# Two transformer graph layers: three stages replaced by one unrolled loop with a chunked softmax and zero matmuls

## Chip, cores and metric

The kernel runs on one core of a Trainium2 chip. The metric is device time in microseconds. Times are given as the median of the runs shown; the profile is of one further execution. TensorE's clock has two levels in these traces, 1.2 and 2.4 GHz, shown as a granted clock of 0.50 and 1.00.

## What is computed

Four graph networks in sequence on 3125 nodes with 128 features and 50,000 edges (`src`, `dst`), each followed by a residual and a layer norm: relation convolution, GCN, GATv2, and two transformer convolutions. The change concerns the last two:

```python
def transformer_conv(x, edge_index, Wq, bq, Wk, bk, Wv, bv, Ws, bs):   # H = 4 heads, C = 32
    q, k, v = (x @ Wq + bq), (x @ Wk + bk), (x @ Wv + bv)              # each N x H x C
    alpha = einsum('ehc,ehc->eh', q[dst], k[src]) / sqrt(C)
    amax = segment_max(alpha, dst)
    ealpha = exp(alpha - amax[dst])
    denom = segment_sum(ealpha, dst)
    out = segment_sum((ealpha / denom[dst])[..., None] * v[src], dst)
    return out.reshape(N, H * C) + x @ Ws + bs
h = relu(transformer_conv(x, ...)); out = transformer_conv(h, ...)
```

## The kernel before

The edges are sorted into 416 pairs. A pair is up to 128 edges (one per partition) whose destinations lie in one window of 125 nodes; there are 25 windows. `m.pair_src` and `m.pair_dst` hold source row and destination inside the window, `m.pair_win_i` the window. Four pairs (G = 4) are a group: 104 groups. What a pair needs of its destination nodes is fetched, and what it gives them is added, by a matmul with a one-hot matrix of edges against nodes.

Each transformer layer is five blocks one after the other (`build`, L1857). `conv_nodes` (L1691) computes q, k, v and the skip part and writes k and v to `kv_table` in DRAM. Then:

- `conv_scores` (L1735). GpSimd gathers k and v rows, one indirect DMA for each pair, into eight slots of `got` (L917); it may run eight groups ahead and waits for a slot's reader. SyncE puts the v half aside into `v_rows` (L938). VectorE makes bf16 one-hots `hot` (L927); TensorE transposes them (L1801), ScalarE copies them to `hot_t` as f32 (L1787), and TensorE multiplies them with q to give `q_b` (L1814; an f32 matmul is two passes, so four pairs are eight instructions). VectorE multiplies `q_b` by the gathered k (L1775), reduces (L1778) and scales (L1780). `q_b`, `hot_b` and `hot_t` have two buffers each.
- `segment_softmax` (L94): the maximum of each destination over all 416 pairs and four heads (1664 columns) by transposes, scans and two broadcasting matmuls (L131), then exp.
- `conv_sums` (L1007), in groups of eight pairs: load `v_rows` back, one-hots `hot` (L1064), messages `msg` = v times weight (L1068), and on TensorE the sums: an f32 matmul with the message (L1092), a bf16 matmul of 12 columns with the weights in three bf16 parts (L1093), and after every second pair a 512-column bf16 matmul of zeros (L1097). The next group's vector work runs beside them.
- `conv_finish` (L1819) divides and adds.

Each engine works through its own list in order; semaphores order the engines among each other. `segment_softmax` is also used by the GAT layer, `gcn_nodes` (L835) prepares the GCN layer.

Of the kernel before, what the change touches and what calls it, by code (L numbers as in the profile page):

```python
# [20 lines left out]
Q, W = 125, 25  # L21
# [9 lines left out]
YS, Y_EARLY, SL = 6, 6, 24  # L31
# [5 lines left out]
assert TILES * P >= E and FULL + W <= PAIRS and Q * W == N  # L37
# [51 lines left out]

def nodes(ap):  # L90
    return ap.rearrange("(w q) d -> q w d", q=Q)

def segment_softmax(nc, m, acc=None):  # L94
# [3 lines left out]
    with ExitStack() as ctx:  # L98
# [12 lines left out]
        alpha = m.alpha[:, :, :].rearrange("l h p -> l (h p)")  # L111
# [34 lines left out]
        def _(dve):  # L146
# [12 lines left out]
            link(v.tensor_copy(topf, high[:, 0:cols]))  # L159
# [18 lines left out]
            link(v.tensor_tensor(less, m.alpha[:, :, :], top[:, :, :], ALU.subtract))  # L178
# [7 lines left out]
def common(m, sb):  # L186
# [14 lines left out]
    m.alpha = sb("alpha", [P, H, PAIRS])  # L201
# [307 lines left out]
def relation_layer(nc, m, y_table):  # L509

    with ExitStack() as ctx:  # L511
# [19 lines left out]
        same = m.alpha  # L531
        pens = m.small[:, :, :].rearrange("l p k -> l (p k)")
        start_pen, end_pen = (pens[:, k * H * PAIRS:(k + 1) * H * PAIRS].rearrange("l (h p) -> l h p", h=H) for k in range(2))
# [32 lines left out]
        def _(dve):  # L566
# [69 lines left out]
            for h in range(H):  # L636
                go(v.tensor_copy(start_pen[:, h, :], ps[2][:, 0:PAIRS]))
                go(v.tensor_copy(end_pen[:, h, :], ps[3][:, 0:PAIRS]))
# [22 lines left out]
            go(v.tensor_scalar(m.leader[:, :], start_pen[:, 0, :], -1.0, None, ALU.is_lt))  # L661
# [69 lines left out]
        def _(pe):  # L731
# [40 lines left out]
            for k, pen in enumerate((start_pen, end_pen)):  # L772
                flat = pen[:, :, :].rearrange("l h p -> l (h p)")
# [61 lines left out]
def gcn_nodes(nc, m, ins, t_table):  # L835

    with ExitStack() as ctx:
# [4 lines left out]
        tb, hb = [bank(f"t1{i}") for i in range(2)], [bank(f"h1{i}") for i in range(4)]  # L842
        loaded, chain, var_ready, std_ready, x_ready = (sem(n) for n in ("loaded1", "chain1", "var1", "std1", "x1_ready"))
# [4 lines left out]
        def _(sp):  # L848
            sp.dma_start(w1[:, :], ins["L1_gnn_W"]).then_inc(loaded, 16)
            for w in range(0, W, 5):  # L850
                sp.wait_ge(t_ready, w + 5)
                sp.dma_start(nodes(t_table)[:, w:w + 5, :], tmp[:, w:w + 5, :]).then_inc(stored, 16)
            sp.wait_ge(stored, 16 * (W // 5))

# [8 lines left out]

        @block.scalar
        def _(act):
            std_of(nc, act, stats, var_ready, std_ready, 1)
# [6 lines left out]
        def _(pe):  # L873
            pe.wait_ge(x_ready, 1)
# [130 lines left out]

def conv_sums(nc, m, v_rows):  # L1007

    with ExitStack() as ctx:  # L1010
        sb, sem, bank = scope(nc, ctx)
        zeros = sb("zeros", [P, 512], BF16)
        rows = sb("rows", [P, 2, WG, D])
        hot = sb("hot", [P, 2, WG, Q])
        msg = sb("msg", [P, 2, WG, D])
        wts = sb("wts", [P, 2, WG, H])
        hot_b, wts3 = sb("hot_b", [P, 2, WG, Q], BF16), sb("wts3", [P, 2, WG, 3, H], BF16)
        left, zero = sb("left", [P, 2, WG, H]), sb("zero", [P, WG, H])
        sums = bank("sums", (P, 8 * 512))
        dens = 7 * 512  # L1020
        used, zeroed, done, hot_ready, wts_ready, msg_ready = (sem(n) for n in (
            "used", "zeroed", "all_summed", "hot_ready", "wts_ready", "msg_ready"))
        hot_b_ready, parts_ready, chain, zero_ready = (sem(n) for n in ("hot_b_ready", "parts_ready", "parts_chain", "zero_ready"))
        come = [sem("come0"), sem("come1")]
        steps = PAIRS // (2 * WG)
        block = ctx.enter_context(nc.Block())

        @block.sync
        def _(sp):  # L1030
            with sp.Fori(0, steps) as i:
                for b in range(2):
                    sp.wait_ge(msg_ready, 2 * i + (b + 1))
                    sp.dma_start(rows[:, b, :, :].rearrange("l (a j) d -> l a (j d)", a=2),
                                 v_rows[bass.ds(i * 4 + 2 * b, 2), :, :].rearrange("a l n -> l a n")).then_inc(come[b], 16)

        @block.gpsimd
        def _(pool):
            pool.memset(zero[:, :, :], 0.0).then_inc(zero_ready, 1)
            pool.wait_ge(zero_ready, 1)  # L1040
            with pool.Fori(0, steps) as i:
                for b in range(2):
                    g = 2 * i + b
                    pool.wait_ge(wts_ready, g + 1)
                    three_parts(pool, wts3[:, b, :, :, :], wts[:, b, :, :], left[:, b, :, :], zero[:, :, :], chain, g, parts_ready)

        @block.scalar
        def _(act):
            with act.Fori(0, steps) as i:
                for b in range(2):  # L1050
                    act.wait_ge(hot_ready, 2 * i + (b + 1))
                    nc.scalar.copy(hot_b[:, b, :, :], hot[:, b, :, :]).then_inc(hot_b_ready, 1)

        @block.vector
        def _(dve):
            v = nc.vector
# [678 lines left out]
def conv_scores(nc, m, kv_table, v_rows):  # L1735

    with ExitStack() as ctx:
# [24 lines left out]
        def _(dve):  # L1763
            v = nc.vector
            dve.sem_inc(used, 2)
            for b in range(2):
                loop.one_hots(b * G, b)
# [156 lines left out]
```

## Time and profile before

| | us |
|---|---|
| median of three runs | 4879.6 (4878.93 to 4885.05) |
| the profiled execution | 4863.76 |
| its span, first to last instruction | 4862.0 |
| mean granted clock over the span | 0.716 |

The page's busy line counts an engine as busy while an instruction runs; waits, register and semaphore instructions are not in it. Its strips cut the span into 40 slices of 121.5 us. The transformer layers are the slices from the 27th on. A table by stretches says more than the whole-span shares, because the stages have different limits; in the timelines and groups the bracket or the third column is the idle time before an instruction and what ended it.

### The profile page before, as it was taken

To read this page: it belongs to the slowest core of one execution; us is meant where nothing else is said; L and a number is where in the kernel's file an instruction comes from. 1 tells how busy PE (TensorE), PEld (TensorE's weight loads), DVE (VectorE), ACT (ScalarE), POOL (GpSimd) and SP (SyncE) were. 2 spreads that over 40 slices of the span, in tenths; PEclk is the share of its full clock that TensorE was granted. 3 is DMA by queue.
4 is the path that set the end of the run, shared out by engine and by line. 5 is a ranking of instruction groups with operands and counts; after the bars stand their busy time and mean duration, and the time that the engine had idled before them with its cause. 6 is when DMAs were issued, how large, how long until landed. Compare 5 with 4: busy or idle time off the path is not lost. (4 is left out here: it accounts for less than half of the span.)

```text
span 4862.0 us, 67990 instructions
## 1 busy us (share of the span) xinstructions
PE 3211.9 (66%) x15577; PEld 2186.9 (45%) x15578; DVE 2813.1 (58%) x9606; ACT 888.8 (18%) x2002; POOL 2734.6 (56%) x3193
## 2 busy tenths in 40 slices
PE   6766677743433259999996998544443984444395
PEld 3235566633333224555543444434443863444284
DVE  8997454431111586676767888744444663444476
ACT  1000111110000021111114777311110211111021
POOL 0016677327777047555535886067774746777373
PEclk9985555555555579999998999855555995555597
DMA  1111122211111104233321221045553435555342
GB/s 61 39 38 45 43 53 53 26 33 51 50 50 50 31 1 103 77 80 79 78 46 43 67 69 49 15 141 153 152 153 93 142 100 143 153 154 154 87 150 83
DMA packets 320800, 387.80 MB, mean 80 GB/s; under 512 B 45989, under 2 KB 230133, under 8 KB 320618
## 3 DMA queue, kind: packets, MB, share of 16 engines
q0 software_dynamic: 80000, 192.10, 15.7%
q1 hardware_dynamic: 240618, 193.80, 13.2%
q14 instruction: 132, 1.08, 0.1%
q8 instruction: 50, 0.82, 0.1%
HBM read 279.89 MB, written 105.84 MB: 79 GB/s over the span
## 5 line engine op out<-in xcount | busy, mean ns | idle before, releaser
L917 POOL DMA_INDIRECT got<-kv_table,pair_src x832 | 814.9, 979 | 497.5 <-issue 252.9
L559 POOL DMA_INDIRECT y_got<-y_table,y_idx x416 | 399.0, 959 | 505.3 <-SPq L511 338.2
L927 DVE TENSOR_TENSOR hot<-pair_dst,iota 128x500 bf16<-128x500 f32 (+1 forms) x424 | 289.3, 683 | 511.0 <-PE sums L990 474.0
L917 POOL DMA_INDIRECT got<-t_table,pair_src x416 | 414.8, 997 | 267.9 <-ACTq L953 141.5
L917 POOL DMA_INDIRECT got<-x_table,pair_src x420 | 398.3, 948 | 286.2 <-issue 283.3
L1801 PE MATMUL hot_b<-ident_b,hot 128*125 128x128 bf16 x840 | 144.1, 327 | 566.5 <-DVE hot L927 566.4
L1439 DVE SCALAR_TENSOR_TENSOR junk<-z,att 128x128 f32<-128x128 f32 x1664 | 381.4, 287 | 179.1 <-PE z L1497 178.1
L1775 DVE TENSOR_TENSOR prod<-q_b,got 128x512 f32<-128x512 f32 x208 | 143.8, 692 | 570.4 <-DMA got<-kv_table,pair_src 538.8
L1493 PE MATMUL z<-gat_wl,got_t 128*128 128x512 f32 x832 | 432.1, 600 | 0.0
L990 PE MATMUL sums<-got,hot 128*125 128x128 f32 x832 | 214.7, 438 | 328.2 <-DMA got<-t_table,pair_src 328.2
L1202 PE MATMUL sums<-msg,hot 128*125 128x512 f32 x832 | 405.3, 636 | 29.2 <-POOL msg L1143 29.2
L1814 PE MATMUL q_b<-acc,hot_t 125*128 x1664 | 420.1, 434 | 0.1
L1801 PEld LDWEIGHTS hot_b<-ident_b,hot 128*125 128x125 bf16 x840 | 105.2, 217 | 628.5 <-DVE hot L927 628.5
L1814 PEld LDWEIGHTS q_b<-acc,hot_t 125*128 125x128 f32 x1664 | 380.1, 333 | 0.5 <-issue 0.5
L990 PEld LDWEIGHTS sums<-got,hot 128*125 128x125 f32 x832 | 184.3, 326 | 359.1 <-issue 359.1
L1497 PE MATMUL z<-xr,hot_t 125*128 x1248 | 336.1, 377 | 0.0
L1188 DVE TENSOR_TENSOR acc<-acc,sums 125x536 f32 x416 | 295.2, 710 | 52.5 <-PE sums L1206 8.3
L1787 ACT CAST hot_t<-hot_b 125x512 f32<-125x512 bf16 x210 | 123.2, 587 | 1010.3 <-PE hot_b L1801 1010.1
L1092 PE MATMUL sums<-msg,hot 128*125 128x128 f32 x1664 | 301.4, 296 | 5.7
L1092 PEld LDWEIGHTS sums<-msg,hot 128*125 128x125 f32 x1664 | 272.0, 188 | 32.5 <-issue 20.3
L1143 POOL TENSOR_TENSOR msg<-rows,wts 128x512 f32<-128x512 f32 x208 | 247.2, 1207 | 36.3 <-DVE wts L1172 33.4
L683 DVE SCALAR_TENSOR_TENSOR hot_w<-iota,src_loc,psum 128x125 f32<-128x125 f32 x416 | 115.2, 339 | 256.9 <-PE psum L795 256.9
(410 smaller groups left out, 6314.8 us busy)
## 6 DMA issues: line engine op xcount, KB each, us to landing
v_rows<-got SPq DMA_DIRECT2D x208, 256.0 KB, 3.2
rows<-v_rows SPq DMA_DIRECT2D x104, 512.0 KB, 3.7
x_rows<-got SPq DMA_DIRECT2D x104, 256.0 KB, 2.6
rows<-x_rows SPq DMA_DIRECT2D x104, 256.0 KB, 2.6
got<-kv_table,pair_src POOLq DMA_INDIRECT x832, 2.9
y_table<-y_stage SPq DMA_DIRECT2D x25, 500.0 KB
got<-x_table,pair_src POOLq DMA_INDIRECT x420
y_got<-y_table,y_idx POOLq DMA_INDIRECT x416, 2.5
```

The lines of the kernel that those rows point to most:

```text
L559: pool.indirect_dma_start(out=got[:, slot, j, :], out_offset=None, in_=y_table[:, :], in_offset=bass.IndirectOffsetOnAxis(ap=m.y_idx[:, co ...
L917: pool.indirect_dma_start(out=self.got[:, slot, j, :], out_offset=None, in_=self.table[:, :], in_offset=bass.IndirectOffsetOnAxis(ap=self. ...
L927: v.tensor_tensor(self.hot[:, b, :, :], bc_last(m.pair_dst[:, cols], Q), bc_mid(m.iota[:, 0:Q], G), ALU.is_equal).then_inc(self.hot_ready, 1)
L990: last = t.matmul(sums[0:Q, bass.ds(ws[j] * D, D)], loop.hot[:, b, j, :], loop.got[:, slot, j, :], start=False, stop=False)
L1092: t.matmul(sums[0:Q, bass.ds(ws[j] * D, D)], hot[:, b, j, :], msg[:, b, j, :], start=False, stop=False)
L1188: v.tensor_tensor(row, row, sums[j][0:Q, 0:H * D + 6 * H], ALU.add).then_inc(read, 1)
L1202: t.matmul(sums[j][0:Q, 0:H * D], hot[:, b, j, :], msg[:, b, j, :], start=True, stop=True)
L1439: last = v.scalar_tensor_tensor(junk[:, j, h, :], z[j][:, h * D:(h + 1) * D], 0.0, m.att[:, h * D:(h + 1) * D], ALU.max, ALU.mult, accum_o ...
L1493: t.matmul(z[j][:, :], got_t[:, b, j, :], m.gat_wl[:, :], start=True, stop=False)
L1497: last = t.matmul(z[j][:, :], hot_t[:, b, j, :], m.xr3[:, bass.ds(ws[j], 1), k, :].rearrange("q o d -> q (o d)"), start=False, stop=(k == 2))
L1801: last = t.transpose(hot_b[b][0:Q, j * P:(j + 1) * P], hot[:, b, j, :], m.ident_b[:, :])
L1814: last = t.matmul(q_b[b][:, j * P:(j + 1) * P], hot_t[:, b, j, :], m.acc[:, bass.ds(w, 1), 0:D].rearrange("q o d -> q (o d)"), start=True, ...
```

## The change

- `conv_scores`, `segment_softmax` (for these two layers) and `conv_sums` go; `conv_layer` takes their place, with all its loops unrolled. The pairs are cut into chunks of 128, 128, 96 and 64 (32, 32, 24 and 16 groups). While chunk c is scored, the messages and sums of chunk c-1 are done between its groups (`sums_due`: one message group for each score group in the second chunk, one or two in the third and fourth); the last chunk's 16 message groups come at the end.
- The one-hot for the query is no longer made, transposed and copied: `gcn_nodes` once writes the destinations as rows `dst_rows` to DRAM, ScalarE's queue loads a row on 125 partitions, and VectorE compares it with the lane (`turn_hot`). `q` is written into one PSUM bank `work`, which also serves the softmax; seven banks hold the sums. The scale moves from the scores into the weights of `conv_nodes`.
- The denominator matmul is f32 with four columns (two passes) in place of the bf16 one with 12; the matmuls use f32 `hot` of 128 columns. The three bf16 parts on GpSimd and the copies on ScalarE go.
- The softmax runs for each chunk (512, 512, 384, 256 columns); a destination that spans chunks is put right at the end with shares (`runs`, `firsts`, `share`, `part`, `rejoin`).
- After the query matmuls of each group TensorE does two matmuls of zeros, 512 columns, bf16.
- `m.alpha` is laid out by chunks, so `gat_scores` has four loops on VectorE in place of one, `segment_softmax` some copies more, and `gcn_nodes` some 35 small VectorE instructions.

```diff
+CHUNK = (128, 128, 96, 64)
 def gcn_nodes(nc, m, ins, t_table, dst_rows):
+            sp.dma_start(dst_rows..., dst_t[:, :, :]).then_inc(dst_stored, 16)
...
-def conv_sums(nc, m, v_rows):
-def conv_scores(nc, m, kv_table, v_rows):
+def sums_due(c, k):
+    if not c:
+        return ()
+    before, n = groups_of(c - 1), len(groups_of(c))
+    return before[k * len(before) // n:(k + 1) * len(before) // n]
+def conv_layer(nc, m, kv_table, dst_rows, v_rows):
...
+        def _(pool):
+            for g in range(groups):
+                slot = g % 8
+                if g >= 8:
+                    pool.wait_ge(used, g - 7)
+                    pool.wait_ge(aside[slot], 16 * (g // 8))
+                for j in range(G):
+                    ... indirect_dma_start(out=got[:, slot, j, :], ...).then_inc(come[slot], 16)
...
+            def load(s):
+                sp.wait_ge(aside[s % 8], 16 * (s // 8 + 1))
+                if s >= 3:
+                    sp.wait_ge(msg_ready, s - 2)
+                sp.dma_start(rows[:, s % 3, :, :], v_rows[s, :, :]...).then_inc(row_back[s % 3], 16)
...
+            def turn_hot(g):
+                dve.wait_ge(row_in[g % 3], 16 * (g // 3 + 1))
+                if g >= 2:
+                    dve.wait_ge(q_done, g - 1)
+                v.tensor_scalar(hot_t[:, g % 2], dst_row[:, g % 3, :]..., m.lane[0:Q, :], None, ALU.is_equal).then_inc(hot_t_ready, 1)
+            def score(c, g):
+                dve.wait_ge(q_done, g + 1)
+                dve.wait_ge(come[g % 8], 16 * G * (g // 8 + 1))
+                v.tensor_tensor(prod[:, g % 2, :, :], work..., got[:, g % 8, :, 0:D], ALU.mult).then_inc(used, 1)
+                if g + 1 < groups:
+                    turn_hot(g + 1)
+                dve.wait_ge(used, g + 1)
+                v.reduce_sum(chunk_view(m.alpha, c)[:, :, at:at + G], prod..., AX).then_inc(scored, 1)
+            def messages(s):
+                if s >= 2:
+                    dve.wait_ge(summed, s - 1)
+                v.tensor_tensor(hot[:, s % 2], m.pair_row..., m.iota..., ALU.is_equal)
+                dve.wait_ge(row_back[s % 3], 16 * (s // 3 + 1))
+                dve.wait_ge(exped, c + 1)
+                v.tensor_tensor(msg[:, s % 2, :, :]..., rows..., w..., ALU.mult).then_inc(msg_ready, 1)
...
+            for c in range(len(CHUNK)):                       # VectorE
+                for k, g in enumerate(groups_of(c)):
+                    score(c, g)
+                    for s in sums_due(c, k):
+                        messages(s)
+                softmax(c)
...
+            def query(c, k, g):                               # TensorE
+                pe.wait_ge(hot_t_ready, g + 1)
+                if g:
+                    pe.wait_ge(used, g)
+                for j in range(G):
+                    last = t.matmul(work[:, j * P:(j + 1) * P], hot_t[:, g % 2, j // 2, j % 2, :], m.acc[...], start=True, stop=True)
+                last.then_inc(q_done, 1)
+                for j in range(G // 2):
+                    t.matmul(psum[:, 0:512], zeros[:, 0:P], zeros[:, :], start=False, stop=False)
+            def add(c, s):
+                pe.wait_ge(msg_ready, s + 1)
+                for j in range(G):
+                    t.matmul(psum[:, bass.ds(ws[j] * D, D)], hot[:, s % 2, j // 2, j % 2, :], msg[:, s % 2, j, :], ...)
+                    last = t.matmul(psum[:, bass.ds(ws[j] * H + dens, H)], hot[:, s % 2, j // 2, j % 2, :], w[:, :, s * G + j - CHUNK_AT[c]], ...)
+                last.then_inc(summed, 1)
...
+            for c in range(len(CHUNK)):
+                for k, g in enumerate(groups_of(c)):
+                    query(c, k, g)
+                    for s in sums_due(c, k):
+                        add(c - 1, s)
+                softmax(c)
+            for s in groups_of(last_chunk):
+                add(last_chunk, s)
```

In `softmax(c)` TensorE and VectorE take turns: transposes, two scans over the columns, transposes back, a copy, a broadcasting matmul, four scans, a second such matmul (it waits until the first has been read, both use `work`), four scans, and some 15 short instructions on the ends.

## Rows read from the trace of the kernel before

**Rows 1.** The page: busy time by engine, and granted clock in slices.

```profile
PE 3211.9 (66%) x15577; PEld 2186.9 (45%) x15578; DVE 2813.1 (58%) x9606; ACT 888.8 (18%) x2002; POOL 2734.6 (56%) x3193
PEclk9985555555555579999998999855555995555597
```

**Rows 2.** Table by stretches: length, busy (instructions) PE, PEld, DVE, ACT, POOL, clock, DMA.

```profile
3181.60:3722.40 540.80, 260.70 (x1252) 230.00 (x1252) 232.18 (x418) 61.60 (x105) 409.38 (x416) 0.50 0.55 151
3722.40:3775.10 52.70, 14.07 (x42) 8.87 (x42) 30.76 (x15) 4.34 (x2) 0.00 (x0) 0.60 0.01 3
3775.10:3968.70 193.60, 185.95 (x1488) 169.42 (x1488) 134.84 (x159) 53.32 (x52) 144.30 (x209) 0.99 0.45 141
3181.60:3968.70 787.10, 460.73 (x2782) 408.29 (x2782) 397.77 (x592) 119.26 (x159) 553.68 (x625) 0.63 0.49 139
4026.20:4810.20 784.00, 462.54 (x2782) 408.79 (x2782) 397.88 (x592) 117.99 (x158) 549.82 (x625) 0.63 0.49 139
```

**Rows 3.** Timeline of one group of scores: start, length, engine, line, idle before.

```profile
3306.68 0.69 DVE L1775 TENSOR_TENSOR prod<-q_b,got 128x512 f32<-128x512 f32 x1 [2.75 <-DMA got<-kv_table,pair_src]
3307.41 0.69 DVE L1778 TENSOR_REDUCE score<-prod 128x16 f32<-128x512 f32 x1
...
3309.96 2.02 PE L1814 MATMUL q_b<-acc,hot_t 125*128 x8
...
3311.80 0.95 POOL L917 DMA_INDIRECT got<-kv_table,pair_src  x1 [0.30 <-issue]
```

**Rows 4.** Groups by form: count, busy us, mean ns, idle before.

```profile
L917 POOL DMA_INDIRECT got<-kv_table,pair_src x832 | 814.9, 979 | 497.5 <-issue 252.9 <-POOLq L55 244.7
L1775 DVE TENSOR_TENSOR prod<-q_b,got 128x512 f32<-128x512 f32 x208 | 143.8, 692 | 570.4 <-DMA got<-kv_table,pair_src 538.8 <-PE q_b L1814 31.6
L927 DVE TENSOR_TENSOR hot<-pair_dst,iota 128x500 f32<-128x500 f32 x106 | 73.6, 695 | 474.0 <-PE sums L990 474.0
L1068 DVE TENSOR_TENSOR msg<-rows,wts 128x1024 f32<-128x1024 f32 x104 | 132.4, 1274 | 4.5 <-DMA rows<-v_rows 4.5
L627 DVE TENSOR_SCALAR pick<-pair_tile,tile_no 98x416 f32<-98x416 f32 x4 | 1.7, 478 | 0.0
```

**Rows 5.** Timeline, PE, GAT node stage: 8-column f32 matmuls.

```profile
1701.46 9.02 PE L1316 MATMUL g_lin<-w_lin,xt 128*125 128x8 f32 x50 [0.40 <-ACT xt L257]
```

**Rows 6.** Table by stretches inside that run, columns as in rows 2.

```profile
1701.43:1703.16 1.73, 1.70 (x16) 1.73 (x16) 0.41 (x1) 0.00 (x0) 0.00 (x0) 1.00 0.00 0
1703.31:1709.89 6.58, 6.58 (x33) 6.58 (x33) 0.00 (x0) 0.00 (x0) 0.00 (x0) 0.50 0.00 0
```

**Rows 7.** Groups in the first transformer layer's softmax, 3722 to 3776 us.

```profile
L155 DVE TENSOR_TENSOR_SCAN carried<-start_turned,sg_low 128x1664 f32<-128x1664 f32 x1 | 3.6, 3621 | 8.5 <-PE sg_low L122 8.5
L131 PE MATMUL sg_high<-top,only 128*128 128x512 f32 (+1 forms) x8 | 5.2, 821 | 2.0 <-DVEq L160 2.0
L126 PE MATMUL sg_high<-ident,carried 128*128 128x128 f32 x13 | 3.0, 425 | 7.4 <-DVEq L157 7.4
L174 DVE TENSOR_TENSOR ends<-ends,first_pen 128x1664 f32<-128x1664 f32 x1 | 1.9, 1892 | 0.0
```

**Rows 8.** Table by stretches: relation sums, scores' start (two), GAT node stage.

```profile
600.00:900.00 300.00, 218.59 (x1265) 188.57 (x1263) 148.76 (x762) 47.29 (x127) 226.88 (x241) 0.50 0.22 53
4027.70:4031.10 3.40, 3.33 (x17) 3.23 (x17) 0.25 (x1) 1.21 (x3) 2.79 (x3) 0.50 0.38 100
4031.10:4034.50 3.40, 0.63 (x6) 0.43 (x4) 1.38 (x2) 0.00 (x0) 2.49 (x4) 1.00 0.33 98
1744.00:1806.00 62.00, 38.81 (x60) 11.97 (x60) 61.04 (x149) 16.19 (x29) 35.29 (x30) 0.81 0.00 0
```

**Rows 9.** Timeline: the first scored group of the first transformer layer.

```profile
3188.49 0.69 DVE L1775 TENSOR_TENSOR prod<-q_b,got 128x512 f32<-128x512 f32 x1 [5.13 <-DMA got<-kv_table,pair_src]
```

**Rows 10.** Timeline: the end of the second layer's sums.

```profile
4809.72 0.46 DVE L1073 TENSOR_REDUCE dens<-sums 125x100 f32<-125x300 f32 x1
```

More of the change, by code:

```diff
@@ L30 @@
 PAD_DST, PAD_SRC = 4000, 3200
[L31 removed]
+YS, Y_EARLY, SL, RB = 6, 6, 24, 104
 BIG = 1.0e30
@@ L36 @@
 BLOCKS = H * PAIRS // P
-assert TILES * P >= E and FULL + W <= PAIRS and Q * W == N
+CHUNK = (128, 128, 96, 64)
+CHUNK_AT = tuple(sum(CHUNK[:c]) for c in range(len(CHUNK)))
+assert TILES * P >= E and FULL + W <= PAIRS and Q * W == N and sum(CHUNK) == PAIRS and all(n % 32 == 0 for n in CHUNK)
 PHASE = itertools.count()
@@ L832, in make_link, with gcn_nodes @@
     return link
-def gcn_nodes(nc, m, ins, t_table):
+def gcn_nodes(nc, m, ins, t_table, dst_rows):
     with ExitStack() as ctx:
@@ L873, in _ @@
         def _(pe):
+            for k in range(PAIRS // RB):
+                last = nc.tensor.transpose(dst_b[0:RB, k * P:(k + 1) * P], m.pair_dst[:, k * RB:(k + 1) * RB], m.ident[:, :])
+            last.then_inc(dst_turned, 1)
+            for b in range(3):
+                at = CHUNK_AT[b + 1] - 1
+                last = nc.tensor.matmul(loc_b[:, b:b + 1], m.only127[:, :], m.pair_dst[:, at:at + 1], start=True, stop=True)
+            last.then_inc(loc_ready, 1)
             pe.wait_ge(x_ready, 1)
@@ new lines, in _ @@
+            for slot in range(8):
+                pool.wait_ge(come[slot], 16 * G * (groups // 8))
+        @block.sync
+        def _(sp):
+            loaded = 0
+            def load(s):
+                sp.wait_ge(aside[s % 8], 16 * (s // 8 + 1))
+                if s >= 3:
+                    sp.wait_ge(msg_ready, s - 2)
+                sp.dma_start(rows[:, s % 3, :, :], v_rows[s, :, :].rearrange("l (j d) -> l j d", j=G)).then_inc(row_back[s % 3], 16)
+            for c in range(len(CHUNK)):
+                for k, g in enumerate(groups_of(c)):
+                    sp.wait_ge(come[g % 8], 16 * G * (g // 8 + 1))
+                    sp.dma_start(v_rows[g, :, :].rearrange("l (j d) -> l j d", j=G), got[:, g % 8, :, D:2 * D]
+                                 ).then_inc(aside[g % 8], 16)
+                    if c:
+                        due = sums_due(c, k)
+                        ahead = min(due.stop + 2 if len(due) else loaded, groups_of(c - 1).stop)
+                        while loaded < ahead:
+                            load(loaded)
+                            loaded += 1
+            while loaded < groups:
+                load(loaded)
+                loaded += 1
@@ new lines, in _ @@
+            v.memset(zeros[:, :], 0.0).then_inc(zeroed, 1)
+            turn_hot(0)
+            for c in range(len(CHUNK)):
+                for k, g in enumerate(groups_of(c)):
[3 more added lines that the diff above has]
+                softmax(c)
+            for b in (1, 0):
+                link(v.tensor_scalar(share[:, b, :], firsts[:, b + 1, :], m.span_pen[:, b:b + 1], None, ALU.add))
+                link(v.tensor_tensor(firsts[:, b, :], firsts[:, b, :], share[:, b, :], ALU.max))
@@ L1819, in conv_finish @@
+            for k in range(7):
+                last = t.matmul(psum[:, k * 512:(k + 1) * 512], zeros[:, 0:P], zeros[:, :], start=False, stop=True)
+            last.then_inc(closed, 1)
+            pe.wait_ge(parts_ready, last_chunk)
+            for b in range(last_chunk):
+                last = t.matmul(work[0:Q, b * (D + H):(b + 1) * (D + H)], m.rejoin[:, b, :], part[:, b, :], start=True, stop=True)
+            last.then_inc(rejoined, 1)
 def conv_finish(nc, m, last_layer, out):
```

432 lines of the change are left out of this document (250 added, 182 removed).

## The prediction

> **What bounds the kernel now.** I read the page's strips first: over the last third of the span the granted clock changes between stages at 0.5 and stages near 0.9 [rows 1], so a share of the whole span says nothing about the transformer layers. The table by stretches cuts the first layer into its three stages: scores 540.8 us, softmax 52.7 us, sums 193.6 us, together 787.1 us; the second layer takes 784.0 us [rows 2]. These 1571.1 us are what the change rebuilds; everything else is 3291 us.
>
> The limit of the scores is in one group's timeline: VectorE waits 2.75 us for the gathered rows, not for TensorE [rows 3]. GpSimd's gathers run back to back: 979 ns each [rows 4] and 0.30 us of issue between them [rows 3], 4 x 1.28 = 5.1 us a group; 540.8 / 104 gives 5.2 us, which I use. TensorE runs all of this at a granted clock of 0.50, and that costs nothing. The sums are TensorE's: busy 186 of 193.6 us at 0.99, which is 1.86 us for four pairs [rows 2]. VectorE's work for the next group lies beside it. So the idea has a price tag: sums and softmax (246 us a layer) beside gathers that leave VectorE and TensorE half idle.
>
> **What the new loop does, in order.** TensorE's list is query(g), zeros, add(s), query(g+1). VectorE's is prod(g), turn_hot(g+1), reduce(g), hot(s), msg(s), prod(g+1). add(s) waits for msg(s), which stands behind five vector instructions; query(g+1) is queued behind add(s) although its own inputs have long been ready; prod(g+1) waits for query(g+1). From the second chunk on this is one closed chain with no overlap but the zeros. Behind a waiting TensorE stands the next query; behind a waiting VectorE stand all messages. Gathers, eight groups ahead, are no longer last, nor are the row loads, three groups ahead on SyncE.
>
> The vector leg: prod 0.69, turn_hot 0.53, reduce 0.69, hot 0.70, msg 0.71, four gaps of 0.04: 3.5 us. The lengths come from rows of the same size (L1775, the f32 L927, L1068 with its 1274 ns for 1024 columns), turn_hot from 478 ns for 416 columns (L627) [rows 4], reduce and gap from [rows 3]. For turn_hot the ends are 0.4 and 0.7; I take the value of the nearest kind.
>
> The Trainium skill, page "TensorE: Matmul & The Clock Gate", section "LDWEIGHTS (loading the stationary operand)", gives the load of P columns as P / 1.2, 107 ns for 128 columns whatever the clock. By it the eight small passes would stay at 0.107 at the low level, the sum would fall by 8 x 0.108 x 104 = 90 us a layer, and the result would be 5128 us. The trace disagrees, since the same small passes go from 0.109 to 0.21 when the clock falls [rows 5, 6].
>
> **Which clock.** The zeros can only be there to raise it, so I looked at what loops of this trace got. The relation sums keep TensorE busy 219 of 300 us and stay at 0.50 throughout. At the start of the second layer's scores 3.33 busy of 3.40 us raised it, but in the next 3.4 us TensorE had 0.63 us of work, and it fell again [rows 8]. Most telling is the run of small f32 matmuls: TensorE was busy for every microsecond and the clock fell in the middle of it and stayed at 0.50 for 6.58 us [rows 5, 6]; half of add's slots are such passes. The GAT node stage (4.2 us cycle, some 2 us idle) alternates, mean 0.81 [rows 8]. The new loop leaves TensorE idle for the vector leg less the zeros, 3.5 - 0.86 = 2.6 us at the low level (3.1 at full), after every block, more than that stage. A rise at the end of query and zeros is therefore spent mostly on idle time. I take the low level with rises that save 10 us a layer (bounds 0 and 25). The zeros themselves (two of 0.43 us) lie beside the vector leg and cost nothing; they would cost 0.86 us a group only if VectorE's leg fell below that.
>
> **The sum for a layer.** Cycle: 3.5 + 0.05 + 24 x 0.215 + 0.2 = 8.9 us, against 5.2 for the gathers.
> - First chunk, bound by the gathers: first prod 6.9 us after the start [rows 9], 31 x 5.2 and 1.9 of vector work: 170 us.
> - 72 groups of the later chunks at 8.9: 641. There are 88 message groups in them, so 16 more adds: 55. Together 696 us.
> - Last chunk's sums: 1.4 for the first message, then 16 x 3.44, TensorE bound and at the low level (nothing but adds), plus the shares 2: 58.5 us. Before, the same four pairs cost 1.86.
> - Softmax, all on the chain, nothing runs beside it but gathers. For 512 columns: transposes 2.3, two scans 2.4 (3.62 us for 1664 columns), a copy 0.7, two broadcasts 4.0, eight short scans 3.4, the ends 5.8 (seven of 0.69, from 1.89 for 1664 columns, and shorter ones), some 20 hops of 0.07: 20 us [rows 7]. The fixed part of a vector instruction, 0.15 us, is an estimate from the 512 and 1024 column rows [rows 4]. For 384 and 256 columns 17 and 13.5: 70.5 us in all, where one softmax of 1664 columns took 52.7 with its block's ends [rows 2].
> - Close: seven zero matmuls 3, parts, windows and rejoin 5, copy 3.5 and the rest: 12 us (before, copy and reduction at the end were 4 [rows 10]).
>
> 170 + 696 + 58.5 + 70.5 + 12 - 10 = 997 us, twice 1994, against 1571: +423. Outside the layers: `gat_scores` is full on TensorE for its loop (its own limit), so the split vector loop hides; conv_nodes' two scalings 0.5 each layer; the longer copies in the GAT softmax 1; the 35 small instructions of `gcn_nodes`, some 10 us beside the store of `t_table`, taken as 3 (0 to 10). Together +5. Span 4862 + 428 = 5290, execution 1.8 more, and the median stood 15.8 above the profiled execution: **5308 us**. Own bounds of this case: low 5237 (turn_hot at 0.4, more rises, cheaper softmax), high 5397 (gaps of 0.12 and turn_hot 0.7 on the chain).
>
> **Rivals.**
> 1. The clock stays at 2.4 GHz: each block of query, zeros and add keeps it up. Cycle 3.5 + 0.05 + 24 x 0.109 + 0.2 = 6.4; layer 170 + 484 + 31 + 61 + 10 = 756, 4826 us, faster by 1.1%. The point from which the chain is faster than before is a cycle of about 6.5 us. For it: the low block is six microseconds long without a gap. Against it: [rows 5, 6, 8].
> 2. It alternates like the GAT node stage, half the work at each level: layer (997 + 756) / 2 = 876, 5067 us.
> 3. The change does what it is laid out for: adds and queries overlap the vector work and the gathers stay the limit. 170 + 72 x 5.2 + last softmax 13.5 + 58.5 + 12 = 628 a layer, 4570 us. Against it stands the order of TensorE's list; it needs query(g+1) ahead of add(s).
> 4. The chain and the low clock as forecast, but small f32 passes keep 0.109 us at the low level: 8 x 0.106 x 104 = 88 us a layer less, 909, 5132 us. Against it: 0.21 for the 8-column passes [rows 5, 6].
> 5. Nothing moves in sum (a clock that is high a little less than always): within 0.2%.
>
> **Chances.** Low clock, chain of 8.9 us: 0.69. Small passes at 0.109: 0.02. Alternating: 0.16. High clock: 0.07. Gather bound: 0.04. No change: 0.02. A measurement of this kernel can tell about 0.2% from no change. Slower 0.87, same 0.02, faster 0.11. The range 5040 to 5400 takes in the likeliest case with its bounds and most of the alternating one; it leaves out the three faster cases and the edges.
>
> **What the profile would show.** Right: VectorE waiting about 5.4 us for TensorE before each prod in the last three chunks, TensorE waiting 2.6 us for msg, a granted clock near 0.5 to 0.6 over the layers, GpSimd waiting for `used`, add's passes 0.21 us apart, and layers near 1000 us. The first chunk still 5.2 us a group. Wrong: a clock of 0.9 or more there, small passes at 0.11 at the low level, VectorE waiting for gathers after the first chunk, or a timeline in which a query runs before the add ahead of it.

## The result and the profile after

| | kernel before | changed kernel |
|---|---|---|
| median | 4879.27 us (4877.56 to 4885.05, 4 runs) | 5243.51 us (5218.7 to 5245.03, 4 runs) |
| span of the profiled execution | 4862.0 us | 5217.0 us |
| first transformer layer | 787.1 us | 951.0 us |
| second transformer layer | 784.0 us | 950.4 us |

The ratio is 1.0732 (of the means; the medians give 1.0747), with a 95% interval of 1.0704 to 1.0760: 7.3% slower. 5308 us was predicted, with a range of 5040 to 5400. The two layers, each from its first gather to the last instruction of the loop that replaces the three stages, cost 330 us more than before. The page has PE and the granted clock in 40 slices, as [rows 1] had:

```profile
PE 3618.6 (69%) x15467; PEld 2484.4 (48%) x15556; DVE 2721.9 (52%) x9731; ACT 658.2 (13%) x1697; POOL 2498.1 (48%) x2775
PEclk9985555555555799999899986555555565555555
```

TensorE's busy share rose from 66% to 69% of a longer span. The stretches of 0.99 that the sums had are gone from the last third: nearly every slice there shows 5 now. The table by stretches of the changed kernel (columns as in [rows 2]) has the first layer, its four chunks from the first to the last product of each, its last 16 adds, and the second layer:

```profile
3203.60:4154.60 951.00, 665.18 (x2722) 557.77 (x2764) 348.30 (x631) 3.70 (x6) 426.45 (x416) 0.53 0.45 129
3212.10:3367.80 155.70, 89.32 (x304) 60.76 (x310) 53.31 (x94) 1.28 (x1) 117.87 (x124) 0.50 0.69 182
3388.00:3648.00 260.00, 186.75 (x790) 161.28 (x806) 89.75 (x156) 0.46 (x1) 143.98 (x138) 0.54 0.51 149
3673.00:3886.00 213.00, 158.49 (x695) 140.22 (x707) 74.64 (x129) 0.57 (x1) 99.32 (x92) 0.56 0.47 137
3912.00:4064.00 152.00, 116.37 (x494) 104.35 (x502) 51.62 (x89) 0.52 (x1) 34.58 (x32) 0.50 0.34 101
4087.20:4141.00 53.80, 52.33 (x245) 52.34 (x246) 20.60 (x32) 0.19 (x1) 0.00 (x0) 0.50 0.22 64
4213.10:5163.50 950.40, 663.17 (x2722) 556.42 (x2764) 347.88 (x631) 2.41 (x5) 425.94 (x416) 0.53 0.46 129
```

The first chunk has 31 steps in 155.7 us, 5.02 us each: the gathers' pace, as before. The second has 31 in 260.0, 8.4 us each, and a typical one is 8.54. The last two chunks have some groups with two adds. Before, scoring took 5.2 us a group and adding 1.86 us [rows 2]: 7.1 us a group for both, one after the other. The loop that was laid out to overlap them takes longer than the two together.

One cycle of the second chunk, from the timeline of all engines (start, length, then the instruction; idle time before it in brackets):

```profile
3504.82 0.69 DVE L1808 TENSOR_TENSOR h<-psum,got 128x512 f32<-128x512 f32 x1 [5.66 <-PE psum L1940]
3505.43 0.48 DVE L1801 TENSOR_SCALAR acc<-dst_row,lane 125x512 f32<-125x512 bf16 x1
...
3505.82 0.68 DVE L1813 TENSOR_REDUCE alpha<-h 128x16 f32<-128x512 f32 x1
...
3506.42 0.68 DVE L1824 TENSOR_TENSOR acc<-pair_row,iota 128x512 f32<-128x512 f32 x1
3507.02 0.69 DVE L1829 TENSOR_TENSOR h<-small,wts 128x512 f32<-128x512 f32 x1
...
3507.84 0.79 PE L1951 MATMUL psum<-h,acc 128*128 128x128 f32 x2 [2.21 <-DVE h L1829]
...
3508.42 0.43 PE L1952 MATMUL psum<-wts,acc 128*128 128x4 f32 x2
...
3511.27 2.05 PE L1940 MATMUL psum<-acc 125*128 x8
...
3513.36 0.69 DVE L1808 TENSOR_TENSOR h<-psum,got 128x512 f32<-128x512 f32 x1 [5.66 <-PE psum L1940]
```

Read it as a relay. VectorE works from 3504.82 to 3507.71 (2.9 us) while TensorE waits 2.21 us for its last instruction, the message. Then TensorE works from 3507.84 to 3513.32 (add, then query) while VectorE waits 5.66 us. In this cycle no add lies beside vector work. Only a group with two adds has some: its second message is made beside the first add. The groups of the page, which answer to [rows 3, 4]:

```profile
L1754 POOL DMA_INDIRECT got<-kv_table,pair_src x832 | 852.4, 1025 | 1122.5 <-DVE h L1808 498.7
L1951 PE MATMUL psum<-h,acc 128*128 128x128 f32 x1664 | 625.3, 478 | 354.3 <-DVE h L1829 354.3
L1808 DVE TENSOR_TENSOR h<-psum,got 128x512 f32<-128x512 f32 x208 | 143.9, 692 | 1035.1 <-PE psum L1940 823.1
```

Before, VectorE waited for the gathers ahead of this product (538.8 us). Now 823.1 of 1035.1 us are waits for the query, and GpSimd in turn waits for the product that frees its slot: the bound moved from GpSimd to the chain between VectorE and TensorE.

### The profile page after: what moved, and what is told of

The parts are those of the page before. It is cut to its first block and busy times, and to the rows that moved or that the text cites. A ratio compares the mean times of both kernels' runs of the same rounds, so it can differ in the third digit from the quotient of the medians.

```text
span 5217.0 us, 63682 instructions
## 1 busy us (share of the span) xinstructions
PE 3618.6 (69%) x15467; PEld 2484.4 (48%) x15556; DVE 2721.9 (52%) x9731; ACT 658.2 (13%) x1697; POOL 2498.1 (48%) x2775
## 5 line engine op out<-in xcount | busy, mean ns | idle before, releaser
L1754 POOL DMA_INDIRECT got<-kv_table,pair_src x832 | 852.4, 1025 | 1122.5 <-DVE h L1808 498.7
L1951 PE MATMUL psum<-h,acc 128*128 128x128 f32 x1664 | 625.3, 478 | 354.3 <-DVE h L1829 354.3
L1808 DVE TENSOR_TENSOR h<-psum,got 128x512 f32<-128x512 f32 x208 | 143.9, 692 | 1035.1 <-PE psum L1940 823.1
L1951 PEld LDWEIGHTS psum<-h,acc 128*128 128x128 f32 x1664 | 431.8, 318 | 483.0 <-issue 483.0
L969 POOL DMA_INDIRECT got<-t_table,pair_src x416 | 431.2, 1037 | 271.3 <-ACTq L1005 144.8
L1940 PE MATMUL psum<-acc 125*128 x1664 | 428.0, 439 | 143.7 <-DVE acc L1801 134.0
L1940 PEld LDWEIGHTS psum<-acc 125*128 125x128 f32 x1664 | 376.4, 331 | 209.5 <-issue 209.5
L1952 PEld LDWEIGHTS psum<-wts,acc 128*128 128x128 f32 x1664 | 441.0, 324 | 0.0
L979 DVE TENSOR_TENSOR hot<-pair_dst,iota 128x500 f32<-128x500 f32 (+1 forms) x212 | 144.4, 682 | 496.7 <-PE sums L1042 491.4
L1952 PE MATMUL psum<-wts,acc 128*128 128x4 f32 x1664 | 348.0, 280 | 0.0
L1117 ACT ACTIVATE msg<-rows,wts 128x128 f32<-128x128 f32 x832 | 254.1, 387 | 1.4 <-DMA rows<-x_rows 1.4
```

The lines of the kernel that those rows point to most:

```text
L969: pool.indirect_dma_start(out=self.got[:, slot, j, :], out_offset=None, in_=self.table[:, :], in_offset=bass.IndirectOffsetOnAxis(ap=self. ...
L1754: pool.indirect_dma_start(out=got[:, slot, j, :], out_offset=None, in_=kv_table[:, :], in_offset=bass.IndirectOffsetOnAxis(ap=m.pair_src[: ...
L1940: last = t.matmul(work[:, j * P:(j + 1) * P], hot_t[:, g % 2, j // 2, j % 2, :], m.acc[:, bass.ds(ws[j], 1), 0:D].rearrange("q o d -> q (o ...
L1951: t.matmul(psum[:, bass.ds(ws[j] * D, D)], hot[:, s % 2, j // 2, j % 2, :], msg[:, s % 2, j, :], start=False, stop=False)
L1952: last = t.matmul(psum[:, bass.ds(ws[j] * H + dens, H)], hot[:, s % 2, j // 2, j % 2, :], w[:, :, s * G + j - CHUNK_AT[c]], start=False, s ...
```

## The experiments

Every ratio is to the kernel before, run beside it. In the first set (without zeros, twelve zeros, and the query ahead with and without zeros) that one took 4861 us. The other sets ran on other chips, where the gather loops of every kernel that has a profile pause now and then, and the kernel before took 5377 to 5379 us; why they pause is open. From these sets I use stretches that hardly wait for gathers, and ratios only within the set.

### Without the zeros

```diff
                 last.then_inc(q_done, 1)
-                for j in range(G // 2):
-                    t.matmul(psum[:, 0:512], zeros[:, 0:P], zeros[:, :], start=False, stop=False)
```

> The changed kernel without its two matmuls of zeros in each group of four pairs. Theory A (the zeros lie beside the vector leg, and all that they do is a few rises of the clock): the 8.54 us cycle stays and no cycle is shorter, so the mean of the second chunk goes from 8.38 to 8.5 us; a layer gains or loses no more than 3 to 12 us, execution 5235 to 5270 us, granted clock over the layers 0.50 to 0.51. Rival B (the zeros stand on the path, since the adds are queued behind them): each group is shorter by up to 0.86 us, 72 groups and two layers: 124 us less, about 5120 us.

Measured: 5223.55 us, ratio 1.0746 (1.0732 to 1.0761). The second chunk, columns as above:

```profile
3367.60:3632.50 264.90, 169.94 (x744) 160.97 (x744) 89.41 (x156) 0.47 (x1) 144.01 (x138) 0.50 0.51 146
```

31 steps of 8.54 us at a clock of exactly 0.50. Theory A holds: the zeros lie beside VectorE's leg. (The time is below the expected 5235 us because the kernel before took 18 us less in this set.) In the profiled execution of the changed kernel they bought a few short stretches of the high clock (0.54 and 0.56 in the table above), worth 13 us in a layer (967.3 against 954.2 us from the first gather to the normalisation that follows). That execution is the exception: it had a mean clock of 0.673 and took 5218.7 us, while the other three had 0.662 to 0.663, took 5242.8 to 5245.0 us, and are at 1.0745, where the kernel without zeros (clock 0.664) is at 1.0746. In most executions, then, the two zeros bought nothing that can be measured.

### Twelve zeros, and six

```diff
-                for j in range(G // 2):
+                for j in range(12):
```

> Twelve matmuls of zeros in each group instead of two, nothing else. Twelve take 5.2 us at the low clock and 2.6 us at the high one, so TensorE has no idle time to speak of beside a vector leg of 2.9 us. Theory A (the clock is low because TensorE is idle for 2.2 us after every block): the granted clock is 1.0 from the second chunk's start to each softmax, the cycle is 2.9 + 0.05 + 2.6 + 0.2 = 5.75 us, layer 164 + 178 + 146 + 100 + 63 + 93 = 744 us, execution about 4823 us. Rival B (the small f32 passes of the denominators bring the clock down however busy TensorE is, as in the run of 8-column matmuls): the clock is near 0.5, the cycle is TensorE's own 24 x 0.215 + 12 x 0.43 + 0.2 = 10.5 us, layer 1172 us, about 5680 us.

Measured: 4811.58 us, ratio 0.9897 (0.9882 to 0.9913). The table over most of the second chunk, and three rows of TensorE's timeline in it:

```profile
3380.00:3550.00 170.00, 156.38 (x1020) 108.73 (x1017) 81.53 (x142) 0.00 (x0) 128.44 (x125) 1.00 0.74 207
```

```profile
3449.74 2.75 PE L1944 MATMUL psum<-zeros 128*128 128x512 bf16 x12
3452.96 0.48 PE L1951 MATMUL psum<-h,acc 128*128 128x128 f32 x2 [0.47 <-DVE h L1829]
...
3454.76 1.14 PE L1940 MATMUL psum<-acc 125*128 x8
```

The clock is 1.00, the cycle 6.00 us. So rival B falls: TensorE's clock stays up with the small passes in the loop, if the zeros fill nearly all of the vector leg (0.47 us idle instead of 2.21). The first layer took 758.4 us, counted as the 951.0 above. This is rival 1 of the prediction at its price (756 us, 4826 us, faster by 1.1%; here 1.0%), with twelve zeros instead of two. Twelve zeros change two things at once, though: they fill the idle time, and they add ten wide passes to each cycle. The run does not say which of the two holds the clock. The cycle of 6.00 is 0.25 above my 5.75, mostly because TensorE's block took 2.98 us and not 2.8.

```diff
-                for j in range(G // 2):
+                for j in range(6):
```

> The changed kernel with six matmuls of zeros in each group instead of two, in its own order. Two gave a clock of 0.53 and cycles of 8.54 us, twelve gave 0.98 and 6.00 us. Six fill 1.3 us of the 2.9 us vector leg at the high clock and 2.6 us at the low one. Theory A (idle time after a block brings the clock down): at the high clock TensorE is idle for 1.6 us in each cycle and falls again, so it alternates: mean clock 0.6 to 0.85, mean cycle 6.6 to 7.8 us, execution 4930 to 5110 us. Rival B (what counts is only that the zeros raise it once): 0.98 and 6.0 us as with twelve, 4812 us. Rival E (nothing below full cover helps): 0.5, 8.5 us, 5230 us.

> The kernel with six matmuls of zeros in each group once more, because in the first comparison the gather loops ahead of the layers and the first chunk took some 10 to 35% longer in every kernel, so that its ratio of 1.0023 says little of the zeros. In the later chunks it had a mean clock of 0.80 to 0.87 and cycles of 6.8 us. With a first chunk of 157 us its layer should be 883 - 66 = 817 us, execution 2 x 146 below the kernel without zeros (967 us a layer): ratio to before 1.0746 - 0.062 = 1.013 if the later chunks come out as there.

Measured: 5390.95 us, ratio 1.0023 (1.0006 to 1.004), and again 5399.66 us, 1.0053 (1.0032 to 1.0075). The second chunk of the one and of the other:

```profile
3767.50:3977.70 210.20, 158.69 (x910) 123.76 (x927) 89.30 (x156) 0.48 (x1) 133.49 (x124) 0.84 0.60 174
```

```profile
3765.80:3978.00 212.20, 162.62 (x909) 124.60 (x926) 89.56 (x156) 0.50 (x1) 131.26 (x124) 0.83 0.60 173
```

Mean cycles of 6.8 us, with a clock of 0.83 and 0.84 between the two levels: the alternation of theory A. The first chunk was no shorter in the second set of these (217 us), so the expected 1.013 had no case to be tested in. Two zeros give 8.4 us a cycle, six 6.8, twelve 6.0.

### The query ahead of the add

```diff
             for c in range(len(CHUNK)):
-                for k, g in enumerate(groups_of(c)):
-                    query(c, k, g)
+                chunk = groups_of(c)
+                query(c, 0, chunk[0])
+                for k, g in enumerate(chunk):
+                    if g + 1 in chunk:
+                        query(c, k + 1, g + 1)
                     for s in sums_due(c, k):
                         add(c - 1, s)
```

> The changed kernel with query(g+1) and its two matmuls of zeros ahead of add(s) in TensorE's list, nothing else. Theory A (the 8.54 us are a closed chain that TensorE's order makes): the adds now run beside VectorE's five instructions, the cycle is the longer of TensorE's own work (at the low clock 24 x 0.215 + 0.86 = 6.0 us) and the gathers (5.05 us), so between 5.05 and 6.2 us by the share of the high clock; layer 713 to 803 us, execution 4760 to 4945 us. Rival B (the chain is closed by something else, a wait of VectorE for rows or of the adds for their messages): the cycle stays above 7.5 us, execution above 5150 us.

Measured: 4572.25 us, ratio 0.9408 (0.9394 to 0.9423): 5.9% faster than before, where the changed kernel is 7.3% slower, by the order of one list. First the whole first layer, then inside it a stretch right after a softmax, the rest of the second chunk, and the last adds; under it VectorE's product among the groups of the execution:

```profile
3180.30:3821.80 641.50, 481.24 (x2766) 408.09 (x2764) 351.40 (x631) 3.69 (x6) 419.44 (x416) 0.69 0.68 192
3371.00:3401.00 30.00, 27.79 (x223) 25.08 (x223) 23.71 (x42) 0.00 (x0) 23.45 (x22) 1.00 0.92 266
3405.00:3515.00 110.00, 86.91 (x535) 77.78 (x535) 61.25 (x106) 0.00 (x0) 84.71 (x84) 0.79 0.79 222
3765.00:3810.00 45.00, 45.00 (x207) 43.21 (x206) 14.22 (x22) 0.00 (x0) 0.00 (x0) 0.50 0.19 53
```

```profile
L1808 DVE TENSOR_TENSOR h<-psum,got 128x512 f32<-128x512 f32 x208 | 143.5, 690 | 406.9 <-DMA got<-kv_table,pair_src 354.1 <-PE psum L1940 51.0 <-DVE small L1876 1.3
```

VectorE's wait for the query fell from 823.1 to 51.0 us, and the gathers are the bound again. The closed chain was made by TensorE's order; rival B falls. This is rival 3 of the prediction, 628 us a layer. Measured are 638.4 us, counted as the 951.0 above (the row's 641.5 go on to the normalisation). That 4572 us is so near its 4570 is in part luck: two layers are 21 us longer than priced, and the kernel before took 18 us less in this set. Theory A holds, but the time came out below its 4760 to 4945 us because I had held each cycle to the gathers' 5.05 us. GpSimd gathers on through each softmax, and the groups after it run from that stock until it is used up: in the 30 us row VectorE did 42 instructions, five for each group, so 3.6 us a group, while GpSimd gathered 22 pairs, 5.5 groups. The first two chunks with the softmax between them take (3514.9 - 3188.2) / 63 = 5.2 us a group, about the gathers' rate.

### The same order without zeros

> As the kernel with query(g+1) ahead of add(s), and without the zeros. Theory A: in this order the zeros are no longer beside other work, so at the low clock leaving them out shortens the cycle by 0.86 us to 5.2 to 5.5 us; layer 760 us, execution about 4856 us, granted clock 0.50 to 0.6. Rival B (the zeros hold the clock in this order): without them the kernel is slower than with them, by up to the difference between 6.0 and 5.05 us in 72 groups, 137 us in both layers.

The edits are the last one and the first. Measured: 4743.85 us, ratio 0.9763 (0.9748 to 0.9778). The same two stretches:

```profile
3371.00:3401.00 30.00, 30.00 (x144) 30.00 (x142) 16.64 (x30) 0.00 (x0) 22.99 (x24) 0.50 0.88 243
3405.00:3515.00 110.00, 110.00 (x517) 110.00 (x517) 63.88 (x109) 0.00 (x0) 85.07 (x82) 0.50 0.82 226
```

Rival B holds, by more than I had allowed: 172 us slower than with zeros, where 137 was my most, since with zeros a group can take less than the 5.05 us that I had put as its floor. Theory A had the clock right (0.50) but not that the zeros would raise it. TensorE is busy for 110 of 110 us and is granted 0.50 throughout, with a cycle of 5.12 us that is its own 24 slots. With two matmuls of zeros in each group, and less busy time (86.91 of 110), the longer stretch had 0.79 and the shorter one 1.00. In this order two zeros are worth 3.6% of the kernel, in the changed kernel's own order nothing that can be measured. And a busy TensorE is not enough for the high clock: it matters which passes it is busy with. The list with the zeros settles the other half as well: it holds the same passes as the changed kernel, and with less idle time between them it got 0.79 to 1.00 instead of 0.54.

The Trainium skill, page "TensorE: Matmul & The Clock Gate", section "Why this matters for your kernels", advises to keep TensorE busy without a break to get the full clock. By the rows above that is not sufficient here: no idle time in 110 us, and half the clock.

### Wide small passes

Each denominator matmul moves 128 columns of the weights instead of 4, so that the denominators are another than the reference's; stationary tile and number of passes are the same.

```diff
-                    last = t.matmul(psum[:, bass.ds(ws[j] * H + dens, H)], hot[:, s % 2, j // 2, j % 2, :],
-                                    w[:, :, s * G + j - CHUNK_AT[c]], start=False, stop=False)
+                    last = t.matmul(psum[:, bass.ds(ws[j] * H + dens, D)], hot[:, s % 2, j // 2, j % 2, :],
+                                    wts[:, c % 2, 0:P], start=False, stop=False)
```

In the order with the query ahead and without any zeros:

> query(g+1) ahead of add(s) and no zeros at all, but each denominator matmul moves 128 columns of the weights instead of 4, with the same stationary tile and the same number of passes. The denominators, and with them the output, are another than the reference's. With 4 columns this order without zeros ran at 0.50 with TensorE busy 154.9 of 156.0 us, 4744 us. Theory C (the four-column passes hold the clock down, because little moves in them): the clock is 0.9 or more in the later chunks and 1.00 in the last 16 adds, which take 1.75 us each (27 us less in a layer); 4572 - 54 = about 4518 us. Rival D (the clock rises only for the bf16 zeros, or the f32 passes hold it down by themselves): 0.50 throughout, 5.12 us a group, about 4744 us. If wide passes cost more slots than small ones, the cycle at the same clock shows it.

Measured: 5165.1 us, ratio 0.9602 (0.9565 to 0.9639). The fourth chunk and the last adds:

```profile
4205.00:4232.00 27.00, 25.93 (x211) 25.25 (x211) 23.50 (x41) 0.00 (x0) 0.00 (x0) 0.94 0.64 180
4258.00:4282.00 24.00, 24.00 (x218) 24.00 (x217) 16.80 (x26) 0.00 (x0) 0.00 (x0) 1.00 0.40 122
```

With not one matmul of zeros between them, the last adds run at 1.00, in 1.79 us each; the same 16 slots with small passes take 3.41 us at 0.50, equally busy. So theory C holds and rival D falls: the four-column passes are what held the clock down in the stretches without idle time. A slot costs the same for 4 and for 128 columns: 1.79 / 16 = 0.112 us.

And in the changed kernel's own order, with its two zeros:

> The changed kernel in its own order, with its two matmuls of zeros, but each denominator matmul moves 128 columns of the weights instead of 4 (the denominators, and with them the output, are another than the reference's). Theory A (in this order TensorE is idle for 2.2 us in every cycle of 8.54 us, and that alone holds the clock down): clock 0.5 to 0.7 in the later chunks outside the last 16 adds, cycle mean 7.5 to 8.5 us, only the last adds gain 27 us a layer; ratio to before 1.05 to 1.062. Theory C (the four-column passes hold it down in this order too, the idle time does not matter): clock above 0.9, cycle 5.75 us, layer about 720 us, ratio about 0.97.

Measured: 5379.97 us, ratio 0.9999 (0.998 to 1.0019). The second chunk, and two neighbouring stretches in it:

```profile
3759.30:3974.20 214.90, 131.72 (x789) 117.33 (x806) 89.37 (x155) 0.53 (x1) 132.88 (x124) 0.85 0.60 171
...
3795.50:3805.80 10.30, 4.95 (x38) 4.00 (x37) 5.76 (x10) 0.00 (x0) 6.07 (x6) 1.00 0.53 152
3805.80:3809.20 3.40, 3.39 (x16) 3.40 (x17) 0.00 (x0) 0.00 (x0) 2.58 (x3) 0.50 0.81 241
```

Neither theory alone. The clock falls once in every two cycles, which take 6.0 and 7.6 us, mean 6.9. From 8.54 us (263.9 / 31 = 8.5 in the changed kernel where gathers pause, below), wide passes give back 1.6 us; filling the idle time (twelve zeros) gives back 2.5, small passes and all. Both causes are there: with small passes and two zeros the clock almost never rises in this order, and with wide ones it still falls after idle time. This is the alternation of rival 2 of the prediction, but not its half and half: of the passes in these two stretches 38 ran at the high level and 16 at the low one.

### The last adds

In the order with the query ahead, zeros between the last chunk's adds, first two for each add, then four:

```diff
                                     w[:, :, s * G + j - CHUNK_AT[c]], start=False, stop=False)
+                    if j % 2 and c == last_chunk:
+                        t.matmul(psum[:, 0:512], zeros[:, 0:P], zeros[:, :], start=False, stop=False)
```

> query(g+1) ahead of add(s), and besides the two matmuls of zeros of each query one more after every second pair of the last chunk's 16 adds, two for each add. Without them these 16 adds keep TensorE busy without a gap and stay at the low clock, 3.41 us each (16 x 0.213). Theory C (it is not idle time but the share of four-column passes that holds the clock down there, and wide matmuls between them bring it up): 16 x 0.109 + 0.43 = 2.2 us each, 20 us less in a layer, 4572 - 39 = 4533 us. Rival D (adds stay at the low clock whatever stands between them): 3.41 + 0.86 = 4.3 us each, 14 us more in a layer, 4600 us.

```diff
-                    if j % 2 and c == last_chunk:
+                    if c == last_chunk:
```

> query(g+1) ahead of add(s), two matmuls of zeros in each query, and one after every pair of the last chunk's 16 adds: four for each of these adds, where two did not raise the clock (3.89 us per add, against 3.41 without any). Theory C (the four-column passes dilute what TensorE moves; enough wide matmuls bring the clock up): 16 x 0.109 + 4 x 0.216 = 2.6 us per add, 13 us less in a layer than without zeros in the tail, ratio to before about 0.941 - 0.005 = 0.936. Rival D (zeros in the tail only cost): 3.41 + 4 x 0.24 = 4.4 us per add, 15 us more in a layer, ratio about 0.947.

> query(g+1) ahead of add(s), two matmuls of zeros in each query and none in the last adds, once more, for its distance to the kernel with four zeros in each of the last adds. If it runs where the gather loops are slow (before at some 5380 us): the last chunk's end takes 92 us instead of 73, two layers 38 us more than 5216 us, ratio about 0.977. If it runs where before takes 4861 to 4879 us: 0.941 as the first time.

For each, a stretch of the last adds in the table, then two of VectorE's messages in its timeline, one add apart. Two zeros:

```profile
4265.00:4315.00 50.00, 49.04 (x229) 47.66 (x231) 16.79 (x26) 0.00 (x0) 0.00 (x0) 0.50 0.21 59
```

```profile
4287.09 0.68 DVE L1829 TENSOR_TENSOR h<-small,wts 128x512 f32<-128x512 f32 x1
...
4290.98 0.69 DVE L1829 TENSOR_TENSOR h<-small,wts 128x512 f32<-128x512 f32 x1
```

Four zeros:

```profile
4276.00:4306.00 30.00, 29.63 (x259) 28.55 (x263) 16.86 (x27) 0.00 (x0) 0.00 (x0) 1.00 0.35 98
```

```profile
4283.26 0.69 DVE L1829 TENSOR_TENSOR h<-small,wts 128x512 f32<-128x512 f32 x1
...
4285.56 0.68 DVE L1829 TENSOR_TENSOR h<-small,wts 128x512 f32<-128x512 f32 x1
```

An add takes 3.41 us without zeros, 3.89 with two and 2.30 with four. Two were a loss (0.24 us each, and the clock stayed at 0.50), four bring 1.00: more work in two thirds of the time. With two, theory C was wrong (2.2 us expected) and rival D (4.3) was nearer; with four, theory C was right (2.6 expected) and rival D (4.4) falls. Whole kernels: two zeros 0.9763 (0.9732 to 0.9793), none 0.9719 (0.9697 to 0.9741), four 0.9704 (0.9669 to 0.9739). From the last product to the normalisation it is 89 us without and 73 us with four, but the medians (5223.5 and 5216.31 us) differ by less than their spread, since the pauses of the gathers are not alike; where gathers don't pause, this version should by this estimate be some 30 us below 4572 us (twice 16), which was not measured.

### The changed kernel again

> The changed kernel itself once more, with a profile. Expected: ratio to before 1.073, as in the comparison; layers 954 to 967 us. The question is the stage ahead of the layers: in the first profile a gather of gcn_sums took 1037 ns (997 before), which made that stage 16 us longer. Theory A (the gathers differ from run to run): 970 to 1000 ns here, and the first layer's first gather at 3180 to 3185 us instead of 3203.6. Rival B (the layout of the changed kernel makes them slower): again 1030 to 1040 ns and 3200 us.

Measured: 5681.02 us, ratio 1.0561 (1.0516 to 1.0606). The gathers of `gcn_sums`, then the first and the second chunk:

```profile
L969 POOL DMA_INDIRECT got<-t_table,pair_src x416 | 407.8, 980 | 349.1 <-ACTq L1005 166.0 <-issue 121.0 <-remote 62.1
```

```profile
3542.60:3756.20 213.60, 81.47 (x304) 56.54 (x310) 53.88 (x94) 1.28 (x1) 137.92 (x147) 0.56 0.54 154
3779.60:4043.50 263.90, 190.76 (x789) 165.42 (x806) 89.48 (x155) 0.52 (x1) 131.22 (x124) 0.51 0.49 139
```

980 ns: the 1037 ns of the first profile are not of the layout (theory A on this point). The time and the place of the first gather were not as expected, since every gather loop pauses here. That makes a test that I had not planned: the gather-bound first chunk goes from 155.7 to 213.6 us, the second from 260.0 to 263.9. A closed chain of VectorE and TensorE doesn't notice slower gathers. The two kernels are 304 us apart here instead of 364; how much of that the chain explains is not shown, since there is no profile of the kernel before in this set.

## Why the prediction was right, and where it was off

**The mechanism** was right: one serial chain of five vector instructions and 24 slots, TensorE near half clock, the gathers no longer the bound after the first chunk. All views named in advance came out so: VectorE waits 5.66 us (said: 5.4), TensorE 2.21 us (2.6), clock 0.53 (0.5 to 0.6), passes 0.213 us apart, layers of 951 us (near 1000). That the order of TensorE's list closes the chain is shown by moving the query ahead, which alone turns 1.073 into 0.941.

**The vector leg was the mis-sized term**: 2.9 us, not 3.5. I had taken instruction lengths with gaps of 0.04 us. The gap comes from [rows 3], where the reduction waits for the product just ahead of it. In the new list no instruction waits for its direct neighbour, and those of 512 f32 columns start 0.60 us apart although each lasts 0.68; `turn_hot` lasts 0.48, not 0.53. That the missing wait is what lets them start earlier fits both timelines, but no run varies it alone. With TensorE's block 0.1 us longer than I had it, the cycle was 8.54 instead of 8.9 us: 72 x 0.36 = 26 us a layer, and the adds, softmaxes and the rest made up the other 20 of the 997 - 951.

**Slots**: 0.213 us for small and wide passes alike at the low level, 0.112 at the high one, as [rows 5, 6] had said. The first chunk took 5.02 us a group (5.2), and the softmaxes 17 us (8.5 us less than the 25.4 us from product to product) instead of 20 for 512 columns, and by the same count 13.4 instead of 17 for 384 (25.4 less the 12.0 of a group with two adds); the last adds 3.41 us (3.44).

**The clock**: level right, 13 us of rises a layer in the profiled execution (10), and by their clock almost none in the other three. My reasons were two, idle time [rows 8] and the falling clock under small f32 passes [rows 5, 6]. Both are shown: wide passes alone move 8.54 to 6.9 us with the idle time left in; the query ahead removes idle time from the same passes and takes 0.54 to between 0.79 and 1.00. Twelve zeros, which do something of both, move the cycle to 6.0. What each does isn't a sum, and which property of a pass the chip weighs is not settled by these runs.

**Outside the layers** I had +5 us; it was 355 - 330 = +25. 16 of it are the gathers of `gcn_sums` in the profiled execution, 1037 against 997 ns, which later runs don't show. `gcn_nodes` and what precedes it put that loop's start 4 us later (1048.8 to 1052.7 us), where I had 3. The rest is spread over stages.

**The total** was 64.5 us too high: 46 us too much in each layer, 92, less 20 outside, less 9 because the median stood 26.5 us above the profiled span where I had taken 17.6. The measured time lies just above my own low bound of 5237 us.

**The rivals' prices** of two were met by kernels that make them true: high clock 756 us a layer (758 with twelve zeros), gather-bound 628 (638 with the query ahead). The alternation came with six zeros, and with wide passes, but not at its price: their mean cycles are 6.8 and 6.9 us, where half the work at each level would make (8.9 + 6.4) / 2 = 7.65.

## What to carry to other kernels

When two loops are merged so that one hides the other, write down both engines' lists side by side and look for the wait that each list puts ahead of work that is ready. A query behind an add that waits for the newest message made the sum of both loops longer than running them in turn; one step ahead in one list was worth 12%. And a filler on TensorE must be judged by the granted clock of the stretch: two matmuls of zeros did nothing beside 2.2 us of idle time, 3.6% in a list that without them had none, and a loss between adds where four were a gain.

## What was not expected of the hardware

- TensorE granted 0.50 while it was busy 110 of 110 us with f32 passes of 128 and 4 columns; with two 512-column bf16 matmuls in each group, or with the 4-column passes widened to 128 columns, the same list reached 1.00 in some stretches. The run of 8-column passes in [rows 5, 6] had pointed at it.
- Widening a pass from 4 to 128 columns costs no time: 0.112 us a slot at the high clock, the small ones' value in the twelve-zero run (16 slots from 3452.96 to 3454.76 us, 0.1125 each).
- A matmul of zeros between passes at the low clock cost 0.24 us, (3.89 - 3.41) / 2, where I had reckoned with 0.43.
- VectorE starts instructions of 512 columns 0.60 us apart when none waits for its neighbour, while each is recorded as 0.68 us.
